# First-layer expert weights split for two units at a time in a gated cross-attention and mixture-of-experts block

## What is computed

```python
logits = xf @ router_w + router_b
top_p, top_i = jax.lax.top_k(jax.nn.softmax(logits, axis=-1), 2)
top_p = top_p / jnp.sum(top_p, axis=-1, keepdims=True)
gates = jnp.zeros((T, 4)).at[jnp.arange(T)[:, None], top_i].add(top_p)
h = jax.nn.silu(jnp.einsum('td,edf->etf', xf, w1)) * jnp.einsum('td,edf->etf', xf, w3)
out = jnp.einsum('te,etd->td', gates, jnp.einsum('etf,efd->etd', h, w2))
```

## Time and profile before

| what | value |
|---|---|
| median of 3 runs | 521.58 us (520.82 to 522.92) |
| the profiled execution's own time | 519.18 us |
| its span in the trace | 517.4 us |
| instructions in the trace | 11394 |
| ACT roundings `w_hi` of first-layer weights (L930) | 152 |
| DVE subtractions `w_lo` of first-layer weights (L1360) | 152 |
| mean granted TensorE clock over the span | 0.985 of full speed |

### The profile page before, as it was taken

One profiled execution on the slowest core, in us unless ns is written; L12 is line 12 of the kernel. 1 busy time (PEld: TensorE's weight loads), 2 busy tenths in 40 slices (PEclk: granted clock), 3 DMA queues, 4 the chain that ended last, 5 costly groups with the idle time before them and its releaser, 6 DMA issues.

```text
span 517.4 us, 11394 instructions
## 1 busy us (share of the span) xinstructions
PE 481.4 (93%) x3622; PEld 438.0 (85%) x3622; DVE 404.5 (78%) x955; ACT 305.1 (59%) x724; POOL 181.8 (35%) x190
## 2 busy tenths in 40 slices
PE   9989999999977899999999999999999999999991
PEld 7557787776756798999999999999999999998880
DVE  2598988998895488887788788888878888887660
ACT  3045556557445566686666656677666767776750
POOL 1456557368766017162036162022202210222111
PEclk9999999999999799999999999999999999999996
DMA  8999885001102302132013132022112111211110
GB/s 268 357 390 410 352 322 194 1 20 54 54 31 95 82 23 46 41 65 42 22 22 54 54 65 42 23 43 29 27 30 42 21 26 26 31 22 23 21 12 11
DMA packets 32392, 45.13 MB, mean 87 GB/s; under 512 B 9709, under 2 KB 28781, under 8 KB 32109
## 3 DMA queue, kind: packets, MB, share of 16 engines
q1 hardware_dynamic: 24807, 34.66, 19.5%
q0 software_dynamic: 6576, 8.92, 10.1%
q10 hardware_dynamic: 960, 0.94, 0.6%
HBM read 33.50 MB, written 21.82 MB: 107 GB/s over the span
## 4 chain that ended last, share of the span: by engine, by line
PE 41%; DVE 33%; issue 9%; POOL 6%; ACT 5%; DVEq 2%; DMA 1%; ACTq 0%; SPq 0%; POOLq 0%
PE ps_scores L1743 11%; DVE w_lo L1360 7%; PE ps_wide L1763 4%; DVE w_lo L1356 4%; DVE ps_scores L1365 3%; PE ps_misc L1763 3%; PE ps_probT L1743 3%; DVE hid_lo L1369 3%; PE ps_wide L1581 3%; ACT hid_hi L951 2%; PE ps_scores L1792 2%; DVE lowest L1235 2%; DVEq L688 2%; POOL score L1068 2%; DVE score L1224 2%
## 5 line engine op out<-in xcount | busy, mean ns | idle before, releaser
L1144 POOL DMA_INDIRECT out_x<-y_out,meta x35 | 57.0, 1627 | 207.5 <-DVE y_out L1388 202.4
L1360 DVE TENSOR_TENSOR w_lo<-w,w_hi 128x512 fp32r<-128x512 f32 x152 | 104.2, 686 | 15.4 <-ACT w_hi L930 7.9
L1743 PE MATMUL ps_scores<-xt_hi,w_hi 128*128 128x256 f32 x384 | 110.8, 289 | 0.2 <-DVE xt_lo L1374 0.2
L1743 PE MATMUL ps_scores<-xt_lo,w_hi 128*128 128x256 f32 x384 | 108.6, 283 | 0.0
L1743 PE MATMUL ps_scores<-xt_hi,w_lo 128*128 128x256 f32 x384 | 108.6, 283 | 0.0
L930 ACT CAST w_hi<-w 128x512 fp32r x152 | 95.3, 627 | 3.5 <-issue 3.0
L1743 PEld LDWEIGHTS ps_scores<-xt_hi,w_hi 128*128 128x128 f32 x384 | 73.5, 192 | 0.6 <-DVE xt_lo L1374 0.4
L1743 PEld LDWEIGHTS ps_scores<-xt_lo,w_hi 128*128 128x128 f32 x384 | 73.6, 192 | 0.0
L1743 PEld LDWEIGHTS ps_scores<-xt_hi,w_lo 128*128 128x128 f32 x384 | 73.5, 192 | 0.0
L951 ACT CAST hid_hi<-ps_scores 128x256 fp32r<-128x256 f32 x96 | 35.8, 373 | 57.5 <-DVE ps_scores L1365 56.1
L944 ACT ACTIVATE act_g<-ps_scores 128x256 f32<-128x256 f32 (+1 forms) x114 | 42.4, 372 | 21.9 <-PE ps_scores L1743 10.4
(11 more groups left out here) (236 smaller groups left out, 1221.1 us busy)
## 6 DMA issues: line engine op xcount, KB each, us to landing
grouped<-in_pad SPq DMA_DIRECT2D x1, 10296.0 KB
w<-in_L_ffn_w SPq DMA_DIRECT2D x8, 1024.0 KB, 12.9
w2s<-in_L_ffn_w SPq DMA_DIRECT2D x4, 1024.0 KB, 13.6
xg<-grouped SPq DMA_DIRECT2D x16, 256.0 KB, 2.7
out_x<-xall SPq DMA_DIRECT2D x8, 256.0 KB, 2.2
xall<-in_x SPq DMA_DIRECT2D x1, 1024.0 KB, 13.2
xall<-in_x SPq DMA_DIRECT2D x1, 768.0 KB, 7.5
ctxT<-in_ctx_t SPq DMA_DIRECT2D x2, 308.0 KB, 5.2
```

The costliest lines, as they stand in the source:

```text
L1144: pool.indirect_dma_start(out, bass.IndirectOffsetOnAxis(ap=meta[:, s % 2, t, E:E + 1].bitcast(U32), axis=0), y_out[:, s % 2, t, :], None, ...
L1360: dve.tensor_tensor(w_lo[:, f % NB], unit_weights(e, f), w_hi[:, f % NB].bitcast(F32), ALU.subtract).then_inc(w_lo_done, 1)
L1743: mm = pe.matmul(ps_gu[f % NB][:, m, 0:n], lhs, rhs[:, a, c, 0:n], start=(k == 0), stop=(k % (3 * DC) == 3 * DC - 1), skip_group_check=True)
```

## The change

The four places of one unit each become two places of one pair of units each. A rounding and a subtraction handle a pair (128x1024 in place of twice 128x512). They stand at odd units only: at f = 1, 3 for the pairs (4, 5) and (6, 7) of the same slot, at f = 5, 7 for the pairs (0, 1) and (2, 3) of the next. On ACT the rounding stands, as before, between `silu` and `hidden_hi`, on DVE the subtraction after `hidden_lo`. TensorE waits for weights at even units only. Short slots are changed in the same way. Before slot 0 two pairs are made in place of three single units.

```diff
-        w_hi = sb("w_hi", [P, NB, 2 * DC, P], F32R)
-        w_lo = sb("w_lo", [P, NB, 2 * DC, P], F32R)
+        w_hi = sb("w_hi", [P, NB // 2, 2 * DC, 2 * P], F32R)
+        w_lo = sb("w_lo", [P, NB // 2, 2 * DC, 2 * P], F32R)
...
-        def unit_weights(e, f):
-            return w13[:, bass.ds(e, 1), :, f * P:(f + 1) * P].rearrange("p o c n -> p (o c) n")
+        def pair_weights(e, p):
+            return w13[:, bass.ds(e, 1), :, 2 * p * P:2 * (p + 1) * P].rearrange("p o c n -> p (o c) n")
+
+        def unit_of(w, f):
+            return w[:, f // 2 % 2, :, f % 2 * P:(f % 2 + 1) * P]
...
-                def weights_hi(v, e, f):
-
-                    if not (isinstance(v, int) and v < NB):
-
-                        act.wait_ge(up_done, v - NB + 1)
-                    act.copy(w_hi[:, f % NB], unit_weights(e, f)).then_inc(w_hi_done, 1)
+                def weights_hi(s, e, p):
+
+                    if not (is_slot(s, 0) and p < 2):
+
+                        act.wait_ge(up_done, FC * s + 2 * p - 2)
+                    act.copy(w_hi[:, p % 2], pair_weights(e, p)).then_inc(w_hi_done, 1)
...
                         if f % 2 == 0:
                             w2_hi_of(s, e, f // 2)
-                        if f < FC - AHEAD:
-                            weights_hi(u + AHEAD, e, f + AHEAD)
-                        elif not last:
-                            if f == FC - AHEAD:
+                        if f % 2 and f < FC - 3:
+                            weights_hi(s, e, (f + 3) // 2)
+                        elif f % 2 and not last:
+                            if f == FC - 3:
                                 e_after = expert_of(act, s + 1)
-                            weights_hi(u + AHEAD, e_after, f + AHEAD - FC)
+                            weights_hi(s + 1, e_after, (f + 3 - FC) // 2)
                         hidden_hi(u, f, n)
...
-                for f in range(1, AHEAD - 1):
-                    weights_hi(f, e, f)
                 ctxT_copy(B - 1)
                 x_hi(0, 0)
-                weights_hi(AHEAD - 1, e, AHEAD - 1)
+                weights_hi(0, e, 1)
...
-                def weights_lo(v, e, f):
-                    dve.wait_ge(w_hi_done, v + 1)
-                    dve.tensor_tensor(w_lo[:, f % NB], unit_weights(e, f), w_hi[:, f % NB].bitcast(F32), ALU.subtract).then_inc(w_lo_done, 1)
+                def weights_lo(s, e, p):
+                    dve.wait_ge(w_hi_done, FC // 2 * s + p + 1)
+                    dve.tensor_tensor(w_lo[:, p % 2], pair_weights(e, p), w_hi[:, p % 2].bitcast(F32), ALU.subtract).then_inc(w_lo_done, 1)
...
-                def up(u, f, a, n):
-                    pe.wait_ge(w_lo_done, u + 1)
+                def up(s, f, a, n):
+                    u = FC * s + f
+                    if f % 2 == 0:
+                        pe.wait_ge(w_lo_done, FC // 2 * s + f // 2 + 1)
...
-                            wh, wl = (w[:, f % NB, m * DC + c] for w in (w_hi, w_lo))
+                            wh, wl = (unit_of(w, f)[:, m * DC + c] for w in (w_hi, w_lo))
...
-                    pe.wait_ge(w_lo_done, u + 1)
+                    if f % 2 == 0:
+                        pe.wait_ge(w_lo_done, FC // 2 * s + f // 2 + 1)
```

More of the change, by code:

```diff
@@ L1406, in slot @@
                         hidden_lo(u, f, n)
[L1407 to L1410, removed]
+                        if f % 2 and f < FC - 3:
+                            weights_lo(s, e, (f + 3) // 2)
+                        elif f % 2 and not last:
+                            if f == FC - 3:
                                 e_after = expert_of(dve, s + 1)
-                            weights_lo(u + AHEAD, e_after, f + AHEAD - FC)
+                            weights_lo(s + 1, e_after, (f + 3 - FC) // 2)
                         if f == 1 and not first:
@@ L1498, in _ @@
                 e = expert_of(dve, 0)
-                for f in range(AHEAD - 1):
-                    weights_lo(f, e, f)
+                weights_lo(0, e, 0)
                 x_lo(0, 0)
                 residual(B - 1)
-                weights_lo(AHEAD - 1, e, AHEAD - 1)
+                weights_lo(0, e, 1)
                 run_slots(slot, short)
@@ L1770, in slot @@
                         u = FC * s + f
-                        up(u, f, a, tiles_of(s) * P)
+                        up(s, f, a, tiles_of(s) * P)
                         if f >= 2:
@@ L1789, in short_up @@
                         xh, xl = (x[:, a, c, 0:P] for x in (xt_hi, xt_lo))
-                        wh, wl = (w[:, f % NB, c::DC, :] for w in (w_hi, w_lo))
+                        wh, wl = (unit_of(w, f)[:, c::DC, :] for w in (w_hi, w_lo))
                         for i, (lhs, rhs) in enumerate(((xh, wh), (xl, wh), (xh, wl))):
```

## The result

The changed kernel took 535.12 us, the median of 4 runs (534.32 to 537.34), against 522.12 for the kernel before on the same chip. The ratio is 1.0258, with a 95% interval from 1.0219 to 1.0297: 13.0 us slower. The forecast was 539 against a median of 521.6, 17.4 slower.

The account below looks back on a forecast made before the run. The loop between ACT and DVE was taken as the bound, not busy times. The shown 519.18 us + 4.1 (slots 0 to 7) + 7.5 (8 to 15) + 6.2 (short) = 537.0; the median 2.4 higher, so 539, range 525 to 545.

Parts of the forecast that it names:

- The bound: Full slots: the length of the loop between ACT and DVE counts, not busy times; DVE 17.5 us per slot, PE 17.7.
- PE's floor: Full slots: PE's own work, 8 x 2.16 + 0.43 = 17.7 us per slot; DVE would pass it.
- The price of the new shapes: ACT's wide rounding would take 1.05 us and DVE's wide subtraction 1.23 us, in place of two small ones each.
- the wait of 0.67 and the pair of 3.83 to 3.84: Odd units, full slots: DVE's wait before hid_lo up from 0.44 to about 0.67, its pair from 3.67 to 3.84 us.
- Slots 8 to 15: Later full slots: DVE passes PE's floor for good, 8 x 1.0 less some 0.5 in hand, +7.5 us.
- A slot: 3 x 0.17 + 0.50 = +1.0: DVE's loss per full slot: three pairs at +0.17 us and the pair at f = 5 at +0.50.
- my third rival: Only in part: register loads slip into the new stalls, full slots stay near PE's floor; 530.5 us, chance 0.22.
- slots 0 to 7: Earlier full slots, 32 pairs: 13 gain behind routing, 19 lose, less what slot 3's PE bound absorbs; +4.1 us.
- PE would wait at `up` for `w_lo`: Slots 8 to 15: PE waits at up of even units for w_lo, without feeding back into DVE's loop.
- Short slots: Slots 16 to 18: wide operations delay DVE's products; 2.3 us for each of the first two, 1.5 the last, +6.2.
- 0.94, 0.6 and 0.8: Short slots: delays in us at f = 1, 3 and 5 from wide operations ahead of DVE's products for PE's transposes.
- The rule of the Trainium skill: Grouping helps saturated engines, splitting those making bubbles; the 0.44 us wait in DVE's pair put this kernel under the second.

Follow-up runs that it names:

- the early rounding: Against the changed kernel, w_hi got four pair places and ACT rounded pairs at even units, DVE still subtracting pairs at odd units; 522.32 us, ratio 0.9976 to before.
- with units: Pairs rounded at even units with four w_hi places, but DVE subtracting unit by unit again; 521.55 us, ratio 1.0006 to before.
- The kernel with hid_hi first: The changed kernel with ACT's hid_hi ahead of the wide rounding at odd units in full slots; 566.03 us, ratio 1.0875 to before.

## Why the prediction was right, and where it was off

**The bound.** Right for the changed kernel: the loop between ACT and DVE sets the pace of full slots, hardly seen in busy times. In the hardware loop DVE's slot went from 17.6 to 18.1 on the mean and passed PE's floor of 17.7. For the kernel before I had put DVE level with PE; there PE kept its floor, and DVE, at 17.6, was catching up on it. PE's transposes of the next slot's tokens start 17.71 or 17.72 apart seven times running, before:

```profile
393.35 0.60 PE L1730 MATMUL ps_scores<-small,xg 128*128 128x128 f32 x4
411.06 0.60 PE L1730 MATMUL ps_scores<-small,xg 128*128 128x128 f32 x4
```

After the change they are 17.7 to 18.3 apart:

```profile
401.02 0.60 PE L1730 MATMUL ps_scores<-small,xg 128*128 128x128 f32 x4
419.27 0.60 PE L1730 MATMUL ps_scores<-small,xg 128*128 128x128 f32 x4
```

So a slot of DVE shorter than 17.71 is worth nothing there, as the early rounding showed.

**The price of the new shapes.** Right to 0.01 us for both. A rounding of 0.95 queue time gave the wait of 0.67 and the pair of 3.83 to 3.84 as forecast.

**Slots 8 to 15.** Mis-sized: 3.4 in place of 7.5. The failed term is "A slot: 3 x 0.17 + 0.50 = +1.0". It measured +0.5 (17.6 to 18.1), and the splits of tokens came 18.1 apart where 18.5 was forecast. I took DVE's register loads as standing still, and they ran beside the wide subtraction: -0.35 to -0.5 for the last pair in place of +0.17. That is the mechanism of my third rival, in part. In slots 0 to 7 it was 2.1 in place of 4.1; the fourth pairs of slots 0, 4, 6 and 7 shrank by 0.50, 0.52, 0.25 and 0.32, 1.6 in all, which would account for most of it if each counts in full.

**What PE waits for.** Wrong in the detail. I wrote that PE would wait at `up` for `w_lo`. The waits over the loop in the changed kernel name others:

```profile
DVE hid_lo L1370 <- ACT hid_hi L954: 21.8, 28, 1.1
...
PE ps_scores L1745 <- DVE xt_lo L1375: 0.5, 2, 0.3
PEld ps_misc L1765 <- DVE hid_lo L1370: 0.4, 2, 0.2
```

It is the split of the next slot's tokens, which stands behind the wide subtraction at f = 5, and `hid_lo`. No row has PE waiting for `w_lo`. But these rows hold only 0.9 us, and the rest of PE's loss is named by none. The table by stretches shows that loss hardly at all, 17.58 busy of 17.89, because matmuls are listed with 0.28 us and follow each other every 0.12.

**Short slots.** Right in kind. PE's timeline in slot 17, the transposes of units 2, 4 and 6:

```profile
500.34 0.33 PE L1800 MATMUL ps_scores<-small,act_g 128*128 128x128 f32 x1 [0.99 <-DVE act_g L1423]
...
503.54 0.33 PE L1800 MATMUL ps_scores<-small,act_g 128*128 128x128 f32 x1 [0.44 <-DVE act_g L1423]
...
507.54 0.33 PE L1800 MATMUL ps_scores<-small,act_g 128*128 128x128 f32 x1 [1.03 <-DVE act_g L1423]
```

The forecast had 0.94, 0.6 and 0.8. Three other traces with wide pairs at odd units there show 6.6 us lost in all, the forecast being 6.2. The other 1.6 in this execution is the clock, in the last section, and no term of the sum had it.

**The rule of the Trainium skill**, page Perfetto Trace Analysis, section Optimizing Scalar/DVE Operations, has grouping help a saturated engine and splitting help where an engine that isn't saturated makes others wait. The traces here agree with both halves. Grouping gained once nothing waited on it (2.9 us in slots 1 to 7 with the rounding early, DVE being busy for 84% of that stretch with units; in one trace of each). Splitting finished sooner where the operations made the bubble (2.5 us in the short slots).

## What to carry to other kernels

Before merging two small instructions into one, look at what stands behind them in their queue and who waits for it: here 17 us less busy time on two engines became 13 us more in all. What counts is the length of the loop through both engines, and work between two waits of one engine is also cover for the other, so removing it exposes what it hid. The remedy was to give the long instruction a place where its engine idles anyway, with the buffers that this needs. It brought back what the change had lost; that it gains more isn't shown.

## What the runs showed of the hardware

The granted clock fell inside the changed kernel's last short slot, in the table by stretches (PE, PEld, DVE, ACT and POOL busy, then the clock):

```profile
505.00:508.00 3.00, 1.97 (x15) 1.64 (x13) 1.95 (x4) 1.57 (x6) 0.00 (x0) 1.00 0.03 1
508.00:510.00 2.00, 1.21 (x7) 0.90 (x6) 0.74 (x1) 1.12 (x2) 0.00 (x0) 0.84 0.00 0
510.00:512.00 2.00, 2.00 (x9) 1.82 (x9) 0.77 (x2) 0.43 (x2) 0.00 (x0) 0.50 0.00 0
512.00:514.00 2.00, 2.00 (x15) 1.95 (x14) 0.29 (x1) 1.03 (x3) 0.00 (x0) 0.80 0.00 0
```

PE had waited 1.03 us for DVE's product and was busy 3.18 of the 5 us up to 510. From about 509.3 to 512.5 it ran at half of full speed, 1.2 in place of 2.4 GHz, its matmuls listed with 0.41 us in place of 0.28. The kernel with hid_hi first shows the same (0.53 from 523 to 526 us); in both, the stretch from slot 16 on takes 60.5 us, in the three other traces with wide pairs at odd units there 58.9 to 59.0. So the fall goes with a further 1.6 us in two of five executions. That PE's waits bring it on isn't shown: PE waits for DVE's product nine times in that stretch in each of the five, 7.1 to 7.9 us in all, and in three of them the clock stayed at 1.00 to PE's last matmul. The kernel before shows a clock of 1.00 in slot 17.
